# Transformer block, attention stage: the P·V matmuls are held back three steps behind the transposes instead of two

## The chip, the cores and the metric

The kernel runs on the 8 cores of one Trainium2 chip (trn2), every core with the same program and its own data. The time is the device time of the slowest core in microseconds (us), lower is better. Two cores share one batch element: each computes K and V for all 2048 positions of it, and the attention and feed-forward for its own 1024 rows (eight tiles of 128 rows).

## The reference, cut to what matters

```python
def reference(x, wq, wk, wv, wo, w_gate, w_up, w_down):   # x is [4, 2048, 2048]
    h = layernorm(x)
    q, k, v = (split_heads(h @ w.T) for w in (wq, wk, wv))  # 16 heads of 128
    scores = einsum('bhqd,bhkd->bhqk', q, k) / sqrt(128)
    scores = where(causal, scores, -inf)
    attn = softmax(scores)
    x = x + merge_heads(einsum('bhqk,bhkd->bhqd', attn, v)) @ wo.T
    h = layernorm(x)
    return x + (silu(h @ w_gate.T) * (h @ w_up.T)) @ w_down.T
```

## The kernel before, in words

The program is written as five lists of instructions, one for each engine, filled in the order in which the Python code runs. Each engine works its own list in order; an instruction that needs another engine's result is preceded by waits on a counter (`pe`, `dve`, `act`, and some for DMA). A wait for a value that the same engine has already waited for is left out (`Plan.wait`, L139 to L147).

The stages: layer norms, transposes and the Q projection up to about 353 us of the profile; attention from 353 to 1246 us; output projection and second layer norm to about 1370 us; gate and up projections to about 2240 us; down projection to the end.

The attention stage is a loop over 16 heads `h` (L567 to L586). Eight query tiles, called slots, form two groups. Group 0 (slots 0 to 3) sees up to 2048 keys, group 1 (slots 4 to 7) up to 1024. For a head the stage emits, in this order: scores and exponentials of the four slots of group 0; the K projection of the next head (64 matmuls); scores and exponentials of group 1; the V projection of the next head (64 matmuls) and its 16 transposes.

`emit_scores_softmax` (L430) does, for one slot, two or four score matmuls into PSUM banks A0, A1, B0, B1, adds masks by further matmuls (L449), and has ScalarE take the exponential of each pair of banks (L459, up to 1024 columns). A slot can write its scores only when the exponentials of the slot before have freed the banks.

What the change touches is `tpv_steps` (L496). It works on the exponentials of a group that was finished earlier. For each block `j` of 128 keys it makes a step:

- T(j): up to four matmuls of 128 columns (L513) that transpose and normalise the block for each slot, into PSUM bank C when j is even and D when j is odd. T(j) waits until that bank was emptied, that is for the eviction of step j-2 (`cd_free`).
- ev(j): one eviction of the bank into a buffer `pt`, by ScalarE when j is even (L522), by VectorE when j is odd (L526). There are four `pt` buffers, so ev(j) may start only when PV(j-4) has read the buffer (`pt_free`).
- PV(j): one matmul of up to 512 columns (L535), which adds the block's product with V into bank E (group 0) or F (group 1). PV(j) isn't emitted in its own step. It is put on the list `pend_pv`, and a later step emits it right behind its own transposes.

Group 0 has 16 steps (j from 0 to 15), group 1 has 8, and each ends with a `tail` that emits the PVs still held and one eviction of the result by VectorE (L547).

These steps are not run in one piece. They are drained between the scores of another group: of group 0's steps five behind each of slots 4 to 7 (L579), of group 1's steps three behind each of slots 0 to 3 of the next head (L570). So TensorE's order is scores of a slot, some steps, scores of the next slot, some steps. ScalarE's order has the exponentials of a slot ahead of the even evictions of the steps behind that slot. Only the last group 1 of the last head runs alone (L586).

There are 32 such groups: 16 group 0's, 15 group 1's between scores, and the last group 1.

Of the kernel before, what the change touches and what calls it, by code (L numbers as in the profile page):

```python
# [230 lines left out]
def emit_program(nc, P, sb, sbank, dr, phases=5):  # L231
# [3 lines left out]
    def bk(name, lo=0, hi=512):  # L235
        t, base = sbank[name]
        return t[:, base + lo: base + hi]
# [258 lines left out]
    def tpv_steps(h, g, slots):  # L496
        obank = "E" if g == 0 else "F"
        maxJ = JS[slots[0]]
        pend_pv = []
        steps = []  # L500

        def step_j(j):
            valid = [s for s in slots if JS[s] > j]
            nv = len(valid)
            jpar = j % 4
            bank = "C" if j % 2 == 0 else "D"

            t_pt = None
            for sl, s in enumerate(valid):
                w = [diag_tok[s], exp_tok[s]]  # L510
                if sl == 0:
                    w.append(cd_free[bank])
                t_pt = P.do("tensor", lambda e, s=s, j=j, sl=sl, bank=bank: e.matmul(  # L513
                    bk(bank, sl * 128, (sl + 1) * 128),
                    sb["p_sb"][:, P_OFF[s] + j * 128:P_OFF[s] + (j + 1) * 128],
                    sb["diag"][:, s, 0, :], start=True, stop=True), waits=w,
                    inc="pe" if sl == nv - 1 else None)
            for s in valid:
                p_region_free[s] = t_pt
                diag_free[s] = t_pt  # L520
            if j % 2 == 0:
                t_ev = P.do("scalar", lambda e, jpar=jpar, nv=nv, bank=bank: e.copy(  # L522
                    pt[jpar][:, 0:nv * 128], bk(bank, 0, nv * 128)),
                    waits=[t_pt, pt_free[jpar]], inc="act")
            else:
                t_ev = P.do("vector", lambda e, jpar=jpar, nv=nv, bank=bank: e.tensor_copy(  # L526
                    pt[jpar][:, 0:nv * 128], bk(bank, 0, nv * 128)),
                    waits=[t_pt, pt_free[jpar]], inc="dve")
            cd_free[bank] = t_ev
            w = [t_ev]  # L530
            if j == 0:
                w.append(ef_free[obank])

            def _pv(j=j, nv=nv, jpar=jpar, w=tuple(w)):
                t_pv = P.do("tensor", lambda e, h=h, j=j, nv=nv, jpar=jpar, obank=obank, maxJ=maxJ: e.matmul(  # L535
                    bk(obank, 0, nv * 128), vtm[h % 2][:, j, :],
                    pt[jpar][:, 0:nv * 128], start=(j == 0), stop=(j == maxJ - 1)),
                    waits=list(w), inc="pe")
                pt_free[jpar] = t_pv
            if len(pend_pv) >= 2:  # L540
                pend_pv.pop(0)()
            pend_pv.append(_pv)

        def tail():
            while pend_pv:
                pend_pv.pop(0)()
            t_oev = P.do("vector", lambda e, h=h, g=g, obank=obank: e.tensor_copy(  # L547
                sb["o_fm"][:, h, g * 512:(g + 1) * 512], bk(obank)),
                waits=[P.tok("pe")], inc="dve")
            ef_free[obank] = t_oev  # L550

        for j in range(maxJ):
            steps.append(lambda j=j: step_j(j))
        steps.append(tail)
        return steps
# [352 lines left out]
```

How the kernel before makes its waits and increments, by code:

```python
    def wait(self, eng, tok):  # L139
        sem, v = tok
        if v <= 0:
            return
        if self.waited[eng].get(sem, -1) >= v:
            return
        h = self.sems[sem]
        self.ops[eng].append(lambda e, h=h, v=v: e.wait_ge(h, v))
        self.waited[eng][sem] = v
# [1 line left out]
    def do(self, eng, build, waits=(), inc=None, k=1):  # L149
        for t in _flat(waits):
            self.wait(eng, t)
        if inc is not None:
            self.cnt[inc] += k
            h = self.sems[inc]
            self.ops[eng].append(lambda e, b=build, h=h, kk=k: b(e).then_inc(h, kk))
            return (inc, self.cnt[inc])
        self.ops[eng].append(lambda e, b=build: b(e))
        return None
```

## Time and profile before

| what | value |
|---|---|
| time before, median of 2 runs | 2916.1 us (2913.26 and 2918.93) |
| the profiled execution's own time | 2902.78 us |
| its span, slowest core (core 5) | 2900.5 us (the eight cores: 2890.1 to 2900.5) |
| TensorE matmul busy | 2450.0 us, 84% of the span |
| VectorE busy | 557.7 us, 19% |
| ScalarE busy | 551.8 us, 19% |
| PE's share of the chain that ended last | 79% |

The span runs from the first to the last instruction of one core. PE is TensorE's matmuls and PEld its weight loads, DVE is VectorE, ACT ScalarE, POOL GpSimd. A matmul's record covers its whole way through the array, so records of neighbouring matmuls overlap: two matmuls of 512 columns that follow each other start 0.22 us apart, though each record is 0.38 us long. A line such as "idle 0.17 <-ACT pt L522" says that the engine stood still for 0.17 us and that the ScalarE instruction of line 522 released it. The granted clock is TensorE's, as a share of 2.4 GHz.

### The profile page before, as it was taken

Reading aid. Unit: us, or ns where it says so; the run is one execution under the profiler, and the core shown is the slowest. Engines: PE = TensorE matmul, PEld = TensorE weight load, DVE = VectorE, ACT = ScalarE, POOL = GpSimd, SP = SyncE. Lnnn points to the kernel's source line nnn. Section 1 sums busy time; section 2 is a strip of 40 time slices with the busy share of each in tenths; the row PEclk is TensorE's granted clock in tenths of the full one; section 3 lists DMA queues with packets and bytes.
Section 4 is the critical chain, followed back from the end, with each engine's and each line's share of the span. In section 5 each row is a group of like instructions: output and inputs, shape, how many; then the busy total and the mean of one; then the engine's idle time right before and its main releaser. Section 6 shows DMA issues by size and latency. Waiting matters only on the chain.

```text
span 2900.5 us, 31994 instructions; the slowest of 8 cores (2890.1 to 2900.5 us)
## 1 busy us (share of the span) xinstructions
PE 2450.0 (84%) x12352; PEld 1143.0 (39%) x12352; DVE 557.7 (19%) x978; ACT 551.8 (19%) x1090; POOL 169.2 (6%) x324
## 2 busy tenths in 40 slices
PE   2676788878888888859779999999999999797796
PEld 1233344434444444414334444444444444343342
DVE  4322133333333333303300010001000100000000
ACT  4433223232333333302210000000000000000000
POOL 0000000000000000010000000000000011111110
PEclk9888999999999999958889999999999999898998
DMA  5333211111110101073244444444444445555554
GB/s 172 116 102 80 44 17 21 19 18 20 18 23 15 22 16 23 1 145 116 78 89 73 80 73 80 73 80 73 80 73 80 73 64 75 112 74 112 94 91 91
DMA packets 61491, 196.36 MB, mean 68 GB/s; under 512 B 6944, under 2 KB 6944, under 8 KB 56096
## 3 DMA queue, kind: packets, MB, share of 16 engines
q0 software_dynamic: 46080, 134.24, 28.5%
q1 hardware_dynamic: 15264, 60.07, 6.2%
q8 instruction: 103, 1.69, 0.2%
q14 instruction: 44, 0.36, 0.0%
HBM read 311.72 MB, written 16.78 MB: 113 GB/s over the span
## 4 chain that ended last, share of the span: by engine, by line
PE 79%; ACT 7%; DMA 5%; issue 4%; DVE 4%; SPq 0%; DVEq 0%; ACTq 0%; POOL 0%; POOLq 0%
PE psA L717 8%; PE psB L728 8%; PE psA L394 4%; PE psA L414 4%; PE psA L802 4%; PE psB L394 4%; PE psF L728 4%; PE psB L414 4%; PE psD L717 4%; PE psC L717 4%; PE psE L728 4%; PE psB L802 4%; PE psA L331 2%; DMA x2r<-x2s 2%; PE psB L331 2%
## 5 line engine op out<-in xcount | busy, mean ns | idle before, releaser
L459 ACT ACTIVATE p_sb<-psA,stats 128x1024 bf16<-128x1024 f32 (+3 forms) x128 | 132.4, 1034 | 559.2 <-PE psA L443 290.2
L717 PE MATMUL psA<-h_fm,wg 128*128 128x512 bf16 x1024 | 227.9, 381 | 8.9 <-issue 8.9
L728 PE MATMUL psB<-h_fm,wu 128*128 128x512 bf16 x1024 | 226.2, 379 | 0.0
L717 PE MATMUL psC<-h_fm,wg 128*128 128x512 bf16 x512 | 194.0, 379 | 0.0
L717 PE MATMUL psD<-h_fm,wg 128*128 128x512 bf16 x512 | 194.0, 379 | 0.0
L728 PE MATMUL psE<-h_fm,wu 128*128 128x512 bf16 x512 | 194.0, 379 | 0.0
L728 PE MATMUL psF<-h_fm,wu 128*128 128x512 bf16 x512 | 194.0, 379 | 0.0
L802 PE MATMUL psB<-wd,hidden 128*128 128x512 bf16 x512 | 155.4, 384 | 24.1 <-DVE osb L816 24.1
L802 PE MATMUL psA<-wd,hidden 128*128 128x512 bf16 x512 | 154.5, 383 | 5.6 <-DVE osb L816 3.8
L526 DVE CAST pt<-psD 128x512 bf16<-128x512 f32 x192 | 115.7, 602 | 210.2 <-PE psD L513 210.2
L717 PEld LDWEIGHTS psA<-h_fm,wg 128*128 128x128 bf16 x1024 | 100.7, 98 | 130.8 <-issue 11.3
L728 PEld LDWEIGHTS psB<-h_fm,wu 128*128 128x128 bf16 x1024 | 100.2, 98 | 120.8
L283 PE MATMUL psE<-eye,htm 128*128 128x128 bf16 x192 | 26.9, 290 | 138.1 <-DVE htm L266 131.2
L513 PE MATMUL psC<-diag,p_sb 128*128 128x128 bf16 x704 | 72.5, 221 | 74.8 <-ACT pt L522 72.5
L394 PE MATMUL psA<-h_fm,wkbuf 128*128 128x512 bf16 x512 | 122.1, 400 | 14.2 <-ACT p_sb L459 13.4
L746 DVE TENSOR_TENSOR hidden<-silu,psB 128x512 bf16<-128x512 bf16 x64 | 41.1, 683 | 422.6 <-PE psB L728 422.6
L414 PE MATMUL psA<-h_fm,wvbuf 128*128 128x512 bf16 x512 | 113.1, 379 | 6.3 <-ACT p_sb L459 6.3
L522 ACT CAST pt<-psC 128x512 bf16<-128x512 f32 x192 | 105.0, 547 | 63.4 <-PE psC L513 61.7
L394 PE MATMUL psB<-h_fm,wkbuf 128*128 128x512 bf16 x512 | 113.1, 379 | 0.0
L414 PE MATMUL psB<-h_fm,wvbuf 128*128 128x512 bf16 x512 | 113.1, 379 | 0.0
L739 ACT ACTIVATE silu<-psA 128x512 bf16<-128x512 f32 x64 | 34.7, 594 | 394.9 <-PE psA L717 394.9
L802 PE MATMUL psE<-wd,hidden 128*128 128x512 bf16 x256 | 98.2, 384 | 12.5 <-DVE osb L816 12.5
(124 smaller groups left out, 2985.4 us busy)
## 6 DMA issues: line engine op xcount, KB each, us to landing
wg<-wg_t POOLq DMA_DIRECT2D x64, 512.0 KB, 5.3
wu<-wu_t POOLq DMA_DIRECT2D x64, 512.0 KB, 5.4
wd<-wd_t POOLq DMA_DIRECT2D x128, 256.0 KB, 3.8
xt<-xkv SPq DMA_DIRECT2D x16, 1024.0 KB, 5.5
wqbuf<-wq_t POOLq DMA_DIRECT2D x16, 512.0 KB, 5.4
xt<-xq SPq DMA_DIRECT2D x8, 1024.0 KB, 10.1
wkbuf<-wk_t POOLq DMA_DIRECT2D x16, 512.0 KB, 5.1
wvbuf<-wv_t POOLq DMA_DIRECT2D x16, 512.0 KB, 5.0
```

What stands on the lines that cost most here:

```text
L331: t_mm = P.do("tensor", lambda e, h=h, sp=sp, c=c, bank=bank: e.matmul(bk(bank), sb["wqbuf"][:, c, :], sb["h1q"][:, c, sp * 512:(sp + 1) * ...
L394: t_mm = P.do("tensor", lambda e, h=h, sp=sp, c=c, bank=bank: e.matmul(bk(bank), sb["wkbuf"][:, c, :], sb["h1_fm"][:, c, sp * 512:(sp + 1) ...
L414: t_mm = P.do("tensor", lambda e, h=h, sp=sp, c=c, bank=bank: e.matmul(bk(bank), sb["wvbuf"][:, c, :], sb["h1_fm"][:, c, sp * 512:(sp + 1) ...
L459: t_exp = P.do("scalar", lambda e, s=s, slo=slo, shi=shi, sec=sec, sc_t=sc_t, sstat=sstat: e.activation(sb["p_sb"][:, P_OFF[s] + slo:P_OFF ...
L513: t_pt = P.do("tensor", lambda e, s=s, j=j, sl=sl, bank=bank: e.matmul(bk(bank, sl * 128, (sl + 1) * 128), sb["p_sb"][:, P_OFF[s] + j * 12 ...
L522: t_ev = P.do("scalar", lambda e, jpar=jpar, nv=nv, bank=bank: e.copy(pt[jpar][:, 0:nv * 128], bk(bank, 0, nv * 128)), waits=[t_pt, pt_fre ...
L526: t_ev = P.do("vector", lambda e, jpar=jpar, nv=nv, bank=bank: e.tensor_copy(pt[jpar][:, 0:nv * 128], bk(bank, 0, nv * 128)), waits=[t_pt, ...
L717: t_gmm = P.do("tensor", lambda e, hc=hc, c=c, half=half, par=par, gb=gb: e.matmul(bk(gb[half]), wg[par][:, c, :], sb["h2_fm"][:, c, half ...
L728: t_umm = P.do("tensor", lambda e, hc=hc, c=c, half=half, par=par, ub=ub: e.matmul(bk(ub[half]), wu[par][:, c, :], sb["h2_fm"][:, c, half ...
L739: t_silu[half] = P.do("scalar", lambda e, half=half, gb=gb: e.activation(sb["silu"][:, half * 512:(half + 1) * 512], bk(gb[half]), AF.Silu ...
L746: t_mul = P.do("vector", lambda e, hc=hc, half=half, ub=ub: e.tensor_tensor(sb["hidden"][:, hc, half * 512:(half + 1) * 512], sb["silu"][: ...
L802: t_mm = P.do("tensor", lambda e, qtr=qtr, hc=hc, tt=tt, par=par, bank=bank: e.matmul(bk(bank), sb["hidden"][:, hc, tt * 128:(tt + 1) * 12 ...
```

## The change

One constant of `tpv_steps`. A step that finds at least three held PVs (it was two) emits the oldest behind its own transposes.

```diff
--- before.py
+++ after.py
@@ -537,7 +537,7 @@
                     pt[jpar][:, 0:nv * 128], start=(j == 0), stop=(j == maxJ - 1)),
                     waits=list(w), inc="pe")
                 pt_free[jpar] = t_pv
-            if len(pend_pv) >= 2:
+            if len(pend_pv) >= 3:
                 pend_pv.pop(0)()
             pend_pv.append(_pv)
```

TensorE's list was T(0) T(1) T(2) PV(0) T(3) PV(1) ... and becomes T(0) T(1) T(2) T(3) PV(0) T(4) PV(1) ... The tail emitted two PVs and now emits three. No instruction is added or taken away on any engine, and no buffer.

## Rows read from the trace of the kernel before

**Rows 1.** Windows: the attention stage; busy us and count, then granted clock.

```profile
core 5: us, PE busy (x) PEld busy (x) DVE busy (x) ACT busy (x) POOL busy (x), PEclk, DMA share, GB/s
353.00:1246.00 893.00, 739.04 (x4532) 374.40 (x4532) 289.36 (x582) 299.19 (x576) 14.77 (x28) 0.98 0.10 18
```

**Rows 2.** Waits: who waited for whom, us in total, times, longest us.

```profile
ACT p_sb L459 <- PE psA L443: 290.2, 31, 31.0
PE psC L513 <- ACT pt L522: 72.5, 79, 2.0
PE psF L535 <- ACT pt L522: 21.7, 15, 1.4
PE psD L513 <- DVE pt L526: 8.7, 30, 0.3
```

**Rows 3.** Line 535 (all PVs): VectorE's share of what ended its idle time: us, times.

```profile
  DVE pt L526: 4.3, 16
```

**Rows 4.** Timeline of a group 1 between scores: start us, us long, engine, line.

```profile
809.14 0.39 PE L513 MATMUL psC<-diag,p_sb 128*128 128x128 bf16 x4
809.36 0.39 PE L513 MATMUL psD<-diag,p_sb 128*128 128x128 bf16 x4
...
811.67 0.38 PE L513 MATMUL psC<-diag,p_sb 128*128 128x128 bf16 x4 [1.92 <-ACT pt L522]
...
811.89 0.38 PE L535 MATMUL psF<-pt,vtm 128*128 128x512 bf16 x1
...
812.11 0.59 PE L443 MATMUL psA<-kfm,q_all 128*128 128x512 bf16 x2
812.15 0.59 ACT L522 CAST pt<-psC 128x512 bf16<-128x512 f32 x1 [0.62 <-PE psC L513]
...
812.80 1.11 ACT L459 ACTIVATE p_sb<-psA,stats 128x1024 bf16<-128x1024 f32 x1
...
813.19 0.39 PE L513 MATMUL psD<-diag,p_sb 128*128 128x128 bf16 x4
...
814.52 0.33 PE L513 MATMUL psD<-diag,p_sb 128*128 128x128 bf16 x3 [0.29 <-DVE pt L526]
...
814.89 0.58 ACT L522 CAST pt<-psC 128x512 bf16<-128x512 f32 x1
814.90 0.59 PE L443 MATMUL psA<-kfm,q_all 128*128 128x512 bf16 x2
...
815.59 1.11 ACT L459 ACTIVATE p_sb<-psA,stats 128x1024 bf16<-128x1024 f32 x1
...
818.08 0.34 PE L535 MATMUL psF<-pt,vtm 128*128 128x256 bf16 x2 [1.45 <-ACT pt L522]
```

**Rows 5.** Timeline of a group 0 between scores, TensorE alone.

```profile
836.96 0.38 PE L513 MATMUL psC<-diag,p_sb 128*128 128x128 bf16 x4 [1.53 <-ACT pt L522]
...
837.39 0.39 PE L513 MATMUL psD<-diag,p_sb 128*128 128x128 bf16 x4
...
838.16 0.38 PE L513 MATMUL psC<-diag,p_sb 128*128 128x128 bf16 x4 [0.17 <-ACT pt L522]
...
847.65 0.22 PE L535 MATMUL psE<-pt,vtm 128*128 128x128 bf16 x1 [0.20 <-DVE pt L526]
848.28 4.04 PE L414 MATMUL psA<-h_fm,wvbuf 128*128 128x512 bf16 x18 [0.42 <-ACT p_sb L459]
```

**Rows 6.** Timeline of the last group 1, which runs alone, TensorE.

```profile
1240.59 0.58 PE L513 MATMUL psC<-diag,p_sb 128*128 128x128 bf16 x4 [0.40 <-ACT pt L522]
...
1241.39 0.63 PE L513 MATMUL psD<-diag,p_sb 128*128 128x128 bf16 x4
```

**Rows 7.** Timeline of ScalarE in another head: slot 2's first exponential.

```profile
471.46 1.11 ACT L459 ACTIVATE p_sb<-psA,stats 128x1024 bf16<-128x1024 f32 x1 [1.06 <-PE psA L443]
```

**Rows 8.** Windows behind a group 1, columns as in rows 1.

```profile
527.00:532.80 5.80, 3.45 (x24) 1.87 (x25) 1.54 (x3) 4.66 (x11) 0.00 (x0) 0.95 0.00 0
532.80:538.60 5.80, 5.80 (x21) 2.33 (x22) 1.76 (x7) 0.62 (x2) 0.00 (x0) 0.75 0.01 3
```

## The prediction, made before the changed kernel was run

> **What bounds the kernel now.** I read the page first: TensorE is busy for 84% of the span and makes up 79% of the chain that ended last, so what counts is TensorE's idle time and what stands in front of it. The windows by stage come second. The change lies in the attention stage alone, 893 us long, in which TensorE is busy for 739 us at a granted clock of 0.98 [rows 1]. About 154 us of it are TensorE standing still. The other stages run the same instructions as before.
>
> The view of waits comes third and says where it stands still [rows 2, 3]. The transposes T(j) wait for ScalarE's evictions 79 times, 72.5 us, and for VectorE's 30 times, 8.7 us: 81.2 us. The PV matmuls wait 15 times for ScalarE, 21.7 us, and 16 times for VectorE, 4.3 us: 26.0 us. So a PV waits in 31 places, about once in each of the 32 groups, though there are 384 PVs. Since each group has one wait, it must be the tail, and the timeline shows it: PV(6) of a group 1 after 1.45 us of standing still, PV(15) of a group 0 after 0.20 us [rows 4, 5].
>
> That is the first thing to see. In the middle of a group a PV never waits for its eviction. T(j) needs PSUM bank C or D, and has therefore already waited for ev(j-2). PV(j-2), which follows it, finds its input ready. TensorE works its list in order, so while T(j) stands still nothing behind it can go. The lists before and after differ in which PV follows a transpose, not in what a transpose waits for.
>
> Here a rule of the Trainium skill speaks against the change. "Perfetto Trace Analysis", section "Optimization Strategy", says that a bubble that comes back again and again can mean too little SBUF or PSUM for the next tile. The trace agrees: 81.2 us of such bubbles stand in front of T and are released by the evictions that empty banks C and D. By that rule a longer list of held PVs gives nothing, and a third bank would be needed.
>
> **The change part by part.** It adds and removes nothing. Each group has one PV fewer early (between T(2) and T(3)) and one more late (in the tail). Between them all PVs come one step later. I price one PV of 512 columns at 0.22 us, the distance from its start to that of the next instruction (811.89 to 812.11), and one T of four matmuls at the same 0.22 us (809.14 to 809.36, two T in a row with nothing between them, which is what T(2) T(3) becomes) [rows 4].
>
> *Group 0, 16 times.* Before: T(2) at 836.96, PV(0), T(3) at 837.39, PV(1), T(4) at 838.16 after 0.17 us of idle [rows 5]. After: T(2) at 836.96, T(3) at 837.18 (its bank's eviction began behind T(1) and is over), PV(0), and then T(4), which waits for ev(2). ev(2) hangs on T(2) alone, which hasn't moved, so T(4) stays at 838.16 and the idle before it grows from 0.17 to 0.39 us. Behind T(4) one PV follows as before, so the scores of slot 5 and all else come when they did. In the tail there is one more PV of 512 columns in front of PV(15). PV(15) waits 0.20 us for ev(15), and the V projection that follows waits 0.42 us more for slot 7's exponential (848.28) [rows 5]. The 0.22 us fall into these. Sum: 0.
>
> *Group 1 between scores, 15 times.* T(0) T(1) T(2) are drained behind slot 0, and PV(0) leaves this place, so the scores of slot 1 start at 811.89 and not 812.11. Their exponential gains nothing: it starts at 812.80 because ev(2), ahead of it on ScalarE, ends at 812.74 (812.15 + 0.59) [rows 4]. But TensorE now runs 0.22 us early. T(3) goes from 813.19 to 812.97, ev(3) with it, T(5), which waits for ev(3), from 814.52 to 814.30, and the scores of slot 2 from 814.90 to 814.68. The exponential of slot 2 starts at 815.59. Its scores end at 814.90 + 0.59 = 815.49, and ev(4) ahead of it on ScalarE ends at 814.89 + 0.58 = 815.47. ScalarE went on 0.06 us behind ev(2), so by ScalarE alone it could start at 815.53. The gain is capped at 0.06 us. From there ScalarE is in charge (two exponentials, ev(6)), and PV(6) waits for ev(6) as before (818.08). The additional PV of the tail lies inside the 1.45 us of idle, which the early lead of 0.22 us would have lengthened. Then scores of slot 3, their exponential and the K projection, all 0.06 us earlier. Sum: 15 x 0.06 = 0.9 us gained.
>
> In one head slot 2's exponential was truly late: ScalarE stood idle for 1.06 us before it [rows 7]. There the 0.22 us come through in full, 0.2 us more. Of the 31 times that L459 waited for L443 [rows 2] this is the only one at slot 2; the others are a head's first exponential and slot 3's.
>
> *The last group 1.* It runs alone and at half clock (T and PV 0.43 us). T(3) moves up from 1241.39 to about 1241.0, T(4) then stands about 0.2 us for ev(2), and the tail, which had no idle, can't give it back [rows 6]. Sum: 0.2 us lost.
>
> *Waits and queues.* No wait is added. ev(j) waits for PV(j-4), to have its `pt` buffer free. Before, PV(j-4) stood behind T(j-2); now it stands behind T(j-1), that is directly in front of T(j), for which ev(j) waits anyway. The four buffers are just enough. DMA issues wait for projections, which move by 0.06 us.
>
> The sum is -0.9 - 0.2 + 0.2 = -0.9 us. The profiled execution took 2902.78 us, so it would be 2901.9. It lies 13 us under the median of the runs shown, 2916.1, and against that the sum gives **2915 us**.
>
> Bounds of the unknown parts. If PV(0)'s place were on the path in full in all 31 groups between scores: -31 x 0.22 = -6.8 us. If the tail's additional PV were never covered: +6.8 us. A PV leaves one place and enters another in every group, so I take the value near zero that the rows give.
>
> The clock is the larger unknown. In the stage it is 0.98, so 2% of 893 us or 18 us are lost to stretches at the lower level. Cut into windows of 5.8 us, 16 of 154 show less than 1.00, in eight places. One of these, behind a group 1, shows 0.95 and then 0.75 [rows 8]. Such a fall costs (0.05 + 0.25) x 5.8 = 1.7 us. They come behind groups 1, where TensorE is busy for 3.45 of 5.8 us, but not in every head. The change moves idle time by 0.22 us within a group, without adding to it. I take no change and keep -18 us (no fall left) and +18 us (twice as many) as its bounds.
>
> **The rivals.**
>
> *The held PVs fill the waits, as a longer lookahead is meant to.* If all PV waits went, 26 us: 2890 us. If those of T went too, 107 us: 2809 us, 3.7% faster. For it: the tail's waits are real, and one more ready PV now stands in front of them. Against it: what that PV covers at the end it leaves open at T(3) or T(4), and T waits for a bank. Chance 3% for the first, 1% for the second.
>
> *The clock falls more often.* The idle before T(4) grows from 0.17 to 0.39 us in every group 0. With 18 us more: 2933 us. With a fall of 1.7 us in each of the 31 groups: 2968 us. Over 2%, 58 us, it takes 34 falls, more than there are groups. Against it: behind a longer stop of 1.53 us group 0's matmuls ran on at full pace (T(2) and PV(0) in 0.43 us) [rows 5]. Chance 6%, and 5% for the other sign, down to 2897 us.
>
> On this the Trainium skill, page "TensorE: Matmul & The Clock Gate", section "A second HAM failure mode: psum-queue depth-cycling", says that short stops between groups of matmuls can make the clock swing between its levels. The trace has both, and the change shifts such stops without lengthening their sum.
>
> *The ring of four buffers is too short (the slower side).* If ev(j) came to wait for a PV emitted behind T(j), each of the 256 evictions from j = 4 on would start one PV later: 256 x 0.22 = 56 us, 2972 us, 1.9% slower. It decides from a distance of four steps on. With three, PV(j-4) still stands in front of T(j). Chance 2%.
>
> **How the numbers follow.** The forecast, no change that can be told, has 80%; the rivals 4, 6, 5 and 2%; 3% stay for what I don't see. A measurement of this kernel can tell about 2%, 58 us, from no change. Only the second half of the first rival lies beyond it on the fast side; on the slow side only worse forms of the ring or the clock: faster 1%, within 2% 97%, slower 2%. The range is 2915 us and 13 us to both sides, the distance between the profiled execution and the median, which also takes in the 6.8 us and most of the clock's 18: 2901 to 2929.
>
> **What would show it.** In the profile of the changed kernel T(3) starts 0.22 us behind T(2) in every group. The idle of T for evictions rises from 81 to about 85 us (16 x 0.22 more in front of T(4)), that of PVs for VectorE falls to about 1 us, and that of PVs for ScalarE stays near 22 us. The attention stage stays 893 us long within 2 us. I am wrong if the waits of T fall by tens of us, if evictions are released by L535, or if the stage's clock leaves 0.97 to 0.99.

## The result and the profile after

The change made the kernel slower by a quarter of a per cent: median 2923.3 us against 2914.2 us, ratio 1.0024 with a 95% interval of 1.0012 to 1.0036. (The chip sometimes lowers the clock of a whole die; such executions are in these two medians and left out of every ratio and mean here.) The profiled execution took 2909.99 us, its span is 2907.6 us on core 0, and the eight cores' spans lie between 2895.2 and 2907.6 us, where before they lay between 2890.1 and 2900.5.

The forecast was 2915 us, no change that can be told and a shade faster. The time, 2923.3 us, lies in its range, but the change is clear of noise and goes the other way.

The stage first. Windows of the changed kernel, core 0 (busy us and count by engine, granted clock, DMA share, GB/s):

```profile
core 0: us, PE busy (x) PEld busy (x) DVE busy (x) ACT busy (x) POOL busy (x), PEclk, DMA share, GB/s
353.00:1246.00 893.00, 735.14 (x4416) 373.46 (x4503) 286.50 (x576) 295.91 (x573) 14.77 (x28) 0.97 0.10 18
```

The clock is 0.97 where it was 0.98 [rows 1]. (Both programs have the same matmuls; the counts, 4416 and 4532, differ because records are missing from the trace, so the busy times aren't compared.) The waits of the same core (waiting instruction, releaser, us in total, times, longest):

```profile
ACT p_sb L459 <- DVE kfm L399: 214.8, 14, 15.9
...
PE psC L513 <- ACT pt L522: 77.6, 81, 2.0
...
PE psF L535 <- ACT pt L522: 18.5, 15, 1.2
```

T waits 5 us more for ScalarE and PV 3 us less [rows 2], and in the records of line 535 VectorE's 4.3 us [rows 3] are gone. That is what a matmul moved from the front of a group to its tail does. The first line is new to the story: ScalarE's wait for the K projection, 7.0 us more than before (core 5):

```profile
ACT p_sb L459 <- DVE kfm L399: 207.8, 14, 15.9
```

Its rows one by one, before (core 5) and after (core 0), in ScalarE's timeline. Each row is the first exponential of four slots; "17.33 <-PE" is the first of group 0, behind the V projection, "<-DVE kfm" the first of group 1, behind the K projection:

```profile
808.75 1.11 ACT L459 ACTIVATE p_sb<-psA,stats 128x1024 bf16<-128x1024 f32 x1 [17.33 <-PE psA L443]
835.13 1.11 ACT L459 ACTIVATE p_sb<-psA,stats 128x1024 bf16<-128x1024 f32 x1 [14.20 <-DVE kfm L399]
865.36 1.11 ACT L459 ACTIVATE p_sb<-psA,stats 128x1024 bf16<-128x1024 f32 x1 [17.33 <-PE psA L443]
893.52 1.11 ACT L459 ACTIVATE p_sb<-psA,stats 128x1024 bf16<-128x1024 f32 x1 [15.87 <-DVE kfm L399]
```

```profile
809.68 1.11 ACT L459 ACTIVATE p_sb<-psA,stats 128x1024 bf16<-128x1024 f32 x1 [17.33 <-PE psA L443]
837.41 1.11 ACT L459 ACTIVATE p_sb<-psA,stats 128x1024 bf16<-128x1024 f32 x1 [15.76 <-DVE kfm L399]
867.64 1.11 ACT L459 ACTIVATE p_sb<-psA,stats 128x1024 bf16<-128x1024 f32 x1 [17.33 <-PE psA L443]
895.40 1.11 ACT L459 ACTIVATE p_sb<-psA,stats 128x1024 bf16<-128x1024 f32 x1 [15.80 <-DVE kfm L399]
```

A head has two sides. The K side runs from the first kind of row to the second, the V side from the second to the next first. The K side before takes 835.13 - 808.75 = 26.4 us with a wait of 14.20, and 893.52 - 865.36 = 28.2 us with a wait of 15.87. The second is a head in which TensorE's clock fell to half behind a group 1, so that the projection, which starts here at about 877 us, ran slowly for a while (before, core 5; the window of 2 us ahead of these shows 1.00):

```profile
877.00:879.00 2.00, 1.99 (x5) 0.70 (x6) 1.04 (x6) 0.65 (x2) 0.00 (x0) 0.51 0.00 0
879.00:881.00 2.00, 2.00 (x7) 0.77 (x6) 0.04 (x1) 0.00 (x0) 0.00 (x0) 0.64 0.00 0
```

I measured all sides of all eight cores in this way, 14 K sides and 15 V sides a core:

| kernel | K sides with a fall | K side, full clock / with a fall | V sides with a fall | V side, full clock / with a fall | all 30 sides, mean of 8 cores |
|---|---|---|---|---|---|
| before | 54 of 112 | 26.39 / 27.95 us | 2 of 120 | 30.23 / 31.73 us | 857.3 us |
| after | 79 of 112 | 26.17 / 27.81 us | 21 of 120 | 30.23 / 31.45 us | 862.0 us |

(The table's durations are medians. The 30 sides are these 29 and the first K side, which has no group 1.) So a head at full clock became 0.22 us shorter, 14 x 0.22 = 3.1 us a core, and the clock fell more often. The falls cost (54 x 1.56 + 2 x 1.50) / 8 = 10.9 us a core before and (79 x 1.64 + 21 x 1.22) / 8 = 19.4 us after. 8.5 us lost less 3.1 us gained is 5.4 us; the sides differ by 4.7 us. Of the 8.5 us, 5.7 are K sides and 2.8 are V sides.

These counts are from one execution of each kernel, and its cores aren't independent: in before, five of the eight show a fall in the very same heads. What bears them out over many executions is the granted clock of the whole program, below.

The V side's falls are nearly new: 21 where there were 2. One in the changed kernel, core 0, TensorE's timeline from T(2) of a group 0 on, and the windows over it:

```profile
433.30 0.38 PE L513 MATMUL psC<-diag,p_sb 128*128 128x128 bf16 x4 [1.53 <-ACT pt L522]
433.52 0.39 PE L513 MATMUL psD<-diag,p_sb 128*128 128x128 bf16 x4
433.74 0.38 PE L535 MATMUL psE<-pt,vtm 128*128 128x512 bf16 x1
...
434.50 0.38 PE L513 MATMUL psC<-diag,p_sb 128*128 128x128 bf16 x4 [0.38 <-ACT pt L522]
```

```profile
431.00:434.90 3.90, 1.99 (x24) 1.34 (x23) 1.80 (x3) 2.26 (x4) 0.53 (x1) 1.00 0.62 98
434.90:438.60 3.70, 3.48 (x20) 2.31 (x20) 0.79 (x2) 2.27 (x4) 0.00 (x0) 0.54 0.20 39
```

T(3) follows T(2) by 0.22 us, and the pause ahead of T(4) is 0.38 us where it was 0.17 [rows 5], just as the working had it. Right behind it the granted clock is 0.54, TensorE's lower level of 1.2 GHz for nearly the whole window.

### The profile page after: what moved, and what is told of

It reads as the page before. It is cut to its first block, busy times and chain, and to the rows that moved or that the text cites. A ratio compares the mean times of both kernels' runs of the same rounds, so it can differ in the third digit from the quotient of the medians.

```text
span 2907.6 us, 31738 instructions; the slowest of 8 cores (2895.2 to 2907.6 us)
## 1 busy us (share of the span) xinstructions
PE 2437.7 (84%) x12111; PEld 1143.3 (39%) x12352; DVE 558.0 (19%) x978; ACT 549.9 (19%) x1090; POOL 169.2 (6%) x324
## 4 chain that ended last, share of the span: by engine, by line
PE 78%; ACT 7%; DMA 5%; issue 4%; DVE 4%; SPq 0%; DVEq 0%; ACTq 0%; POOL 0%; POOLq 0%
PE psA L717 8%; PE psB L728 8%; PE psA L394 4%; PE psF L728 4%; PE psD L717 4%; PE psA L414 4%; PE psA L802 4%; PE psB L802 4%; PE psB L394 4%; PE psB L414 4%; PE psC L717 4%; PE psE L728 4%; DMA x2r<-x2s 2%; ACT p_sb L459 2%; PE psA L331 2%
## 5 line engine op out<-in xcount | busy, mean ns | idle before, releaser
L717 PE MATMUL psA<-h_fm,wg 128*128 128x512 bf16 x1004 | 227.8, 382 | 10.8 <-DMA wg<-wg_t 9.6
L717 PE MATMUL psC<-h_fm,wg 128*128 128x512 bf16 x491 | 186.1, 379 | 0.0
L728 PE MATMUL psE<-h_fm,wu 128*128 128x512 bf16 x491 | 186.1, 379 | 0.0
L394 PE MATMUL psA<-h_fm,wkbuf 128*128 128x512 bf16 x502 | 128.5, 417 | 14.7 <-ACT p_sb L459 13.4
L513 PE MATMUL psC<-diag,p_sb 128*128 128x128 bf16 x704 | 72.3, 221 | 80.5 <-ACT pt L522 77.6
L522 ACT CAST pt<-psC 128x512 bf16<-128x512 f32 x192 | 105.0, 547 | 63.0 <-PE psC L513 61.3
L802 PE MATMUL psC<-wd,hidden 128*128 128x512 bf16 x246 | 94.6, 385 | 12.9 <-DVE osb L816 12.9
```

What stands on the lines that cost most here:

```text
L394: t_mm = P.do("tensor", lambda e, h=h, sp=sp, c=c, bank=bank: e.matmul(bk(bank), sb["wkbuf"][:, c, :], sb["h1_fm"][:, c, sp * 512:(sp + 1) ...
L717: t_gmm = P.do("tensor", lambda e, hc=hc, c=c, half=half, par=par, gb=gb: e.matmul(bk(gb[half]), wg[par][:, c, :], sb["h2_fm"][:, c, half ...
L728: t_umm = P.do("tensor", lambda e, hc=hc, c=c, half=half, par=par, ub=ub: e.matmul(bk(ub[half]), wu[par][:, c, :], sb["h2_fm"][:, c, half ...
L802: t_mm = P.do("tensor", lambda e, qtr=qtr, hc=hc, tt=tt, par=par, bank=bank: e.matmul(bk(bank), sb["hidden"][:, hc, tt * 128:(tt + 1) * 12 ...
```

## The experiments

Two theories. *Clock*: the new order itself gains 0.22 us a head; the loss comes from more falls of TensorE's clock. *Path*: the order costs time by itself, and the falls are incidental. If it is the clock, it is still open what calls for it: the 0.2 us more of pause ahead of T(4), the tail, or where a head lies in time. "Mean core span" is the mean over the eight cores of all executions that enter the ratio, with its standard error; it is less noisy than the slowest core's time, by which the ratios go. The changed kernel's is 2903.0 +-0.6 us; before's was 2894.2, 2893.2 and 2895.9 us (all +-0.6 or less) in the three sets of runs, each on another chip. Falls are again counted in one execution of each kernel. The granted clock of the whole program, a mean over the same executions as the spans (errors of 0.0007 or less; the kernels are those of the sections below), tells the same story:

| kernel | granted clock, whole program |
|---|---|
| before, three sets | 0.9465, 0.9462, 0.9458 |
| the changed kernel | 0.9414 |
| two held, filled (two sets) | 0.9509, 0.9507 |
| three held, filled (two sets) | 0.9506, 0.9511 |
| group 0 alone | 0.9426 |
| group 1 alone | 0.9459 |
| whole change, T(4) filled | 0.9469 |
| held to T(4) only | 0.9425 |
| three held late | 0.9430 |
| a head 0.22 us longer | 0.9486 |
| faster than both | 0.9509 |

### Taking the falls away

Idle matmuls in TensorE's pauses, into the PSUM bank (E or F) that the stretch doesn't use. Nothing reads them.

```diff
+    def fill(bank, n, cols=512):
+        for _ in range(n):
+            P.do("tensor", lambda e, bank=bank, cols=cols: e.matmul(
+                bk(bank, 0, cols), eye[:, :], sb["h1_fm"][:, 0, 0:cols],
+                start=True, stop=True), waits=[ef_free[bank]])
...
             pend_pv.append(_pv)
+            if j == 1 and not solo:
+                fill(fbank, 6 if g == 0 else 7)
...
             while pend_pv:
+                if len(pend_pv) == 2 and g == 1 and not solo:
+                    fill(fbank, 5)
                 pend_pv.pop(0)()
...
         emit_combine(h, 0)
         if h + 1 < NH:
+            fill("E", 3)
```

(`fbank` is F in group 0 and E in group 1, `solo` the last group 1. In kernels with these lines L513 becomes L521, L522 L530 and L535 L543; L498 is the idle matmul.) With two PVs held:

> Two PVs held as before the change, and idle matmuls (128x512, into the PSUM bank that the stretch does not use) in TensorE's pauses: 7 behind T(1) of a group 1, 5 ahead of PV(6), 3 ahead of each K projection, 6 behind T(1) of a group 0. Clock theory (the change is slower because the clock falls in more heads, 11 of 14 K sides in its trace against 7 before, 1.6 us each): no K side is longer than 27 us here, the stage's clock is 1.00, and the time is about 10 us below before (7 falls x 1.6), 2904. Path theory (the new order itself costs time; the clock is incidental): the fillers change nothing, 2914, or cost a few us where they are in the way.

With three:

> Three PVs held, and the same idle matmuls. Clock theory: all falls are gone, and what is left of the change is its gain in heads at full clock, 26.2 against 26.4 us on the K side: 15 x 0.2 = 3 us less than d2_warm, about 2901. Path theory: 7 to 9 us more than d2_warm.

Both were run again in another set:

> The kernel with two PVs held and idle matmuls in the pauses, a second time, as the partner of the next two. No falls in the attention stage; mean core span about 9 us below before.

> Three PVs held and idle matmuls in the pauses, a second time. Order alone, with no falls: K sides of 26.17 us against 26.39, so the attention stage is 3 us shorter than with two held, and the mean core span too (within its noise of about 1 us).

| kernel | ratio to before, 95% interval | mean core span | K falls | V falls | K side | all sides |
|---|---|---|---|---|---|---|
| two held, filled | 0.9955 (0.9938 to 0.9973) | 2884.9 +-0.8 us | 0 | 0 | 26.39 us | 846.3 us |
| three held, filled | 0.9974 (0.9951 to 0.9996) | 2882.9 +-1.2 us | 0 | 0 | 26.17 us | 843.3 us |
| two held, again | 0.9953 (0.9923 to 0.9982) | 2885.7 +-1.0 us | 0 | 0 | 26.39 us | 846.3 us |
| three held, again | none (only two executions count) | 2881.6 +-1.1 us | 0 | 0 | 26.17 us | 843.4 us |

No side falls in any core. The pauses filled are seen in TensorE's timeline of three held, filled, core 3. T(2) stood for 1.92 us before; now seven idle matmuls run and 0.41 us are left:

```profile
408.57 1.67 PE L498 MATMUL psE<-h_fm,eye 128*128 128x512 bf16 x7
410.66 0.38 PE L521 MATMUL psC<-diag,p_sb 128*128 128x128 bf16 x4 [0.41 <-ACT pt L530]
```

And the order alone, with no fall in either, is 3 us shorter with three held (846.3 to 843.3 us, and 846.3 to 843.4 in the second set). The path theory, which wanted 7 to 9 us more, is out. The sums close as well: the falls cost 857.3 - 846.3 = 11.0 us before and 862.0 - 843.3 = 18.7 us after the change, 7.7 us more, and 7.7 less the 3.0 of order is the 4.7 us by which the sides differ. By the slowest core's time this 3 us doesn't show: the two kernels' intervals overlap, with three held even on the higher side in the first set. Its profiled execution took 2921.35 us, and its slowest core had a granted clock of 0.78 ahead of the attention stage (up to 353 us) and of 1.00 within it, so that time wasn't lost in the attention stage. The mean core spans lean the way of the 3 us (2.0 and 4.1 us, each with an error of about 1.5, the second with only two executions of three held).

### Which group

```diff
-            if len(pend_pv) >= 2:
+            if len(pend_pv) >= (3 if g == 0 else 2):
```

> Three PVs held in group 0 only, two in group 1. If the longer pause ahead of T(4) of group 0 (0.17 to 0.39 us) is what lowers the clock: slower than before by 6 to 9 us, with heads at full clock 26.4 + 30.2 us. If it is group 1: as before, 2914.

The other kernel has `(3 if g == 1 else 2)`.

> Three PVs held in group 1 only, two in group 0. If group 1 (26.2 us on the K side at full clock, and longer rows of heads with a fall) is the cause: slower than before by 6 to 9 us. If it is group 0: 2 to 3 us faster than before, by 0.2 us a head.

| kernel | ratio, 95% interval | mean core span | K falls | V falls | all sides |
|---|---|---|---|---|---|
| group 0 alone | 1.0020 (1.0005 to 1.0035) | 2902.3 +-0.5 us | 48 of 112 | 53 of 120 | 863.7 us |
| group 1 alone | 1.0015 (0.9996 to 1.0034) | 2894.7 +-1.5 us | 59 of 112 | 1 of 120 | 855.1 us |

Group 0 brings the V sides' falls and 8.1 us of mean core span (2902.3 against 2894.2), group 1 the 0.22 us (K side 26.17 us) and no loss of span (+0.5 +-1.5). I had expected either the full loss or 2 to 3 us of gain from group 1. In the profiled execution its sides are 2.2 us shorter (855.1 against 857.3), with 59 K falls against 54; over all executions no gain shows, and where it went isn't shown.

### The pause ahead of T(4)

The whole change, plus one idle matmul of 0.22 us in that pause:

```diff
-            if len(pend_pv) >= 2:
+            if len(pend_pv) >= 3:
...
+            if g == 0 and j == 4:
+                fill("F", 1)
             t_pt = None
             for sl, s in enumerate(valid):
```

> Three PVs held in both groups, and one idle matmul of 512 columns (0.22 us) in the pause ahead of T(4) of every group 0, which brings TensorE's idle time there back from 0.39 to 0.17 us. Pause theory (the 0.22 us more of idle there is what lowers the clock in group 0's stretch): V sides with a fall go from 21 of 120 in the changed kernel, and 53 in the one with group 0 alone, back to about 2, and the mean span of the cores goes from 2903 to about 2894. Order theory (the falls come from the shifted order or from the head's length, not from this pause): the falls stay, the time stays near the changed kernel's, 1.002 of before.

Measured: V falls 0 of 120, K falls 60 of 112, all sides 855.0 us, mean core span 2890.0 +-0.8 us against 2893.2 +-0.6 of before in the same set, ratio 0.9993 (0.9978 to 1.0009). TensorE's timeline of core 5:

```profile
430.36 0.38 PE L521 MATMUL psC<-diag,p_sb 128*128 128x128 bf16 x4 [1.53 <-ACT pt L530]
430.58 0.39 PE L521 MATMUL psD<-diag,p_sb 128*128 128x128 bf16 x4
430.80 0.38 PE L543 MATMUL psE<-pt,vtm 128*128 128x512 bf16 x1
431.02 0.38 PE L498 MATMUL psF<-h_fm,eye 128*128 128x512 bf16 x1
431.56 0.38 PE L521 MATMUL psC<-diag,p_sb 128*128 128x128 bf16 x4 [0.17 <-ACT pt L530]
```

and the window over this and the following:

```profile
428.00:435.60 7.60, 5.49 (x54) 3.35 (x53) 3.25 (x5) 4.92 (x9) 0.53 (x1) 1.00 0.42 69
```

T(4) starts 1.20 us behind T(2), as in the changed kernel (434.50 - 433.30). Nothing on the path moved; only 0.22 us of idle time became busy, once in each of 16 heads. That took all of the V side's falls away, and the loss with them. The K falls too are 60 here, as good as the 59 of group 1 alone, where the changed kernel had 79. The K sides' part of the cost was 5.7 of 8.5 us, so much of what the pause cost seems to come out on K sides; how a pause on a V side brings a fall behind the next group 1 these runs don't show. The changed kernel itself wasn't run again in this set; each is compared with its own before, 1.0024 and 0.9993, and the two intervals don't overlap.

The same from the other side: three held from T(3) to T(4) only, and two again from T(5) on, so that the tail is as before.

```diff
-            if len(pend_pv) >= 2:
+            if len(pend_pv) >= (2 if g == 1 or j > 4 else 3):
                 pend_pv.pop(0)()
+            if g == 0 and j == 5:
+                pend_pv.pop(0)()
```

> Group 1 as before. Group 0 holds three PVs only from T(3) to T(4) and emits two behind T(5), so that all from there on, the tail too, is as before. Pause theory: the pause ahead of T(4) is 0.39 us, so V sides fall as in the kernel with group 0 alone (53 of 120) and the mean core span is about 8 us above before. Tail theory (what counts is the longer tail or the shift of all PVs): as before.

Measured: V falls 71 of 120, K falls 28 of 112, mean core span 2903.5 +-0.5 us (+10.3), ratio 1.0041 (1.0027 to 1.0056). Core 1, TensorE, and the two windows of 3.7 us from the first exponential of the side on:

```profile
493.26 0.38 PE L513 MATMUL psC<-diag,p_sb 128*128 128x128 bf16 x4 [0.38 <-ACT pt L522]
```

```profile
490.20:493.90 3.70, 1.79 (x21) 1.11 (x19) 1.38 (x2) 2.42 (x5) 0.31 (x1) 0.96 0.71 118
493.90:497.60 3.70, 3.70 (x21) 2.07 (x19) 0.69 (x1) 2.03 (x4) 0.00 (x0) 0.58 0.14 28
```

With the pause there and the tail as before, the falls stay. The tail theory is out for the V sides.

### Where a head lies in time

Three held late in group 0, from T(9) on, with the early part as before:

```diff
-            if len(pend_pv) >= 2:
+            if len(pend_pv) >= (3 if g == 0 and j >= 9 else 2):
```

> Group 1 as before. Group 0 holds two PVs up to T(8) and three from T(9) on, the tail included. Pause theory: V sides fall in 2 to 5 of 120, as before; the held PV(7) moves behind the scores of slot 6, whose exponential found ScalarE idle for 0.9 us, so a V side at full clock gets shorter by up to 0.2 us, 3 us in all. Tail theory: V sides fall in some 50 of 120 and the mean core span is 8 us above before.

And before itself, with a head made 0.22 us longer by one matmul more on TensorE's path:

```diff
+                if c == 0 and sp == 0 and h > 0:
+                    for _ in range(1):
+                        P.do("tensor", lambda e, bank=bank: e.matmul(
+                            bk(bank, 0, 512), sb["wkbuf"][:, 0, :],
+                            sb["h1_fm"][:, 0, 0:512],
+                            start=True, stop=True), waits=w)
+                    w = []
```

> Two PVs held as before; each K projection (from the second head on) starts with one more matmul of 512 columns, on TensorE's path, so that a head is 0.22 us longer and all pauses are the same. If the falls depend only on the pauses: K sides fall in 54 of 112 as before, V sides in 2 of 120, and the kernel is 15 x 0.22 = 3.3 us slower. If they depend also on how long a head is (where it lies in time against the chip's own rhythm): the number of falls changes by more than 15, either way, and the time by more than 5 us from that.

| kernel | ratio, 95% interval | mean core span | K falls | V falls | K / V side, full clock | a head with a K fall |
|---|---|---|---|---|---|---|
| three held late | 1.0039 (1.0022 to 1.0056) | 2900.7 +-0.9 us | 98 of 112 | 0 of 120 | 26.39 / 30.01 us | 57.99 us |
| a head 0.22 us longer | 1.0000 (0.9980 to 1.0021) | 2893.3 +-0.6 us | 26 of 112 | 1 of 120 | 26.60 / 30.23 us | 58.39 us |

"Three held late" is a miss of both theories. The V side has no fall and is 0.22 us shorter, as the pause theory said, but the kernel is 7.5 us slower, because nearly every K side falls, though group 1 wasn't touched. Core 5, ScalarE:

```profile
574.77 1.11 ACT L459 ACTIVATE p_sb<-psA,stats 128x1024 bf16<-128x1024 f32 x1 [17.33 <-PE psA L443]
602.79 1.11 ACT L459 ACTIVATE p_sb<-psA,stats 128x1024 bf16<-128x1024 f32 x1 [15.84 <-DVE kfm L399]
632.79 1.11 ACT L459 ACTIVATE p_sb<-psA,stats 128x1024 bf16<-128x1024 f32 x1 [17.33 <-PE psA L443]
660.96 1.11 ACT L459 ACTIVATE p_sb<-psA,stats 128x1024 bf16<-128x1024 f32 x1 [15.70 <-DVE kfm L399]
```

Head after head 58.0 us apart (632.79 - 574.77), each with a slow K projection. The kernel with a longer head does 3.3 us more work on the path, leaves every pause as it was, and has half as many falls as before (26 against 54), so that the time is the same. Of the two marks set, the falls passed theirs (more than 15), and the time, 3.3 us under the forecast, not its own (more than 5 us). Falls come in rows of heads that follow each other, and the rows are the longer the nearer a head with a fall is to 58.0 us. All kernels that have falls, K sides and V sides apart:

| kernel, side that falls | head with such a fall (both sides) | falls | longest row of heads |
|---|---|---|---|
| a head 0.22 us longer, K | 58.39 us | 26 of 112 | 2 |
| before, K | 58.18 us | 54 of 112 | 5 |
| held to T(4) only, K | 58.18 us | 28 of 112 | 4 |
| group 0 alone, K | 58.15 us | 48 of 112 | 4 |
| group 1 alone, K | 58.04 us | 59 of 112 | 10 |
| the changed kernel, K | 58.04 us | 79 of 112 | 7 |
| whole change, T(4) filled, K | 58.01 us | 60 of 112 | 10 |
| three held late, K | 57.99 us | 98 of 112 | 14 |
| held to T(4) only, V | 58.05 us | 71 of 120 | 10 |
| group 0 alone, V | 57.82 us | 53 of 120 | 7 |
| the changed kernel, V | 57.62 us | 21 of 120 | 2 |

The three rows of V sides have the same pause ahead of T(4) and differ in the length of a head, which may be why they have 21, 53 and 71 falls. So the longer pause brings falls on V sides, and how often they come depends also on how long a head is, within tenths of a microsecond. Why 58.0 us is a bad length isn't shown by these runs. The table is one profile of each kernel, and it has equal or nearly equal lengths with 54 and 28, 59 and 79, 60 and 98 falls, so the length isn't all of it.

### A version faster than both

The pauses filled as above, three held in group 1, and three held from T(9) on in group 0:

```diff
-            if len(pend_pv) >= 2:
+            if len(pend_pv) >= (3 if g == 1 or j >= 9 else 2):
```

> Idle matmuls in the pauses; three PVs held in group 1, and in group 0 from T(9) on. If the gains at full clock add (0.22 us on the K side from group 1, 0.22 us on the V side from the PV that moves behind slot 6's scores): K sides 26.17, V sides 30.01, no falls, attention stage 840 us against 843.3 with three held everywhere and 846.3 with two, and about 0.994 to 0.995 of before. If the falls come back in spite of the idle matmuls: above 846.

Measured: 0.9940 of before (0.9921 to 0.9960), mean core span 2879.3 +-0.5 us against 2895.9. No falls, K side 26.17, V side 30.01, all sides 840.1 us. The gains of both groups add once the clock stays up. Its idle matmuls cost no one a wait. The profile of line 498, core 0 (counts, durations, and then two lists of who waited, both empty):

```profile
L498 PE MATMUL psE<-h_fm,eye x225: 379/379/379, 355.3 to 1196.8; 128*128 128x512 bf16 x113
...
L498 PE MATMUL psF<-h_fm,eye x96: 379/379/379, 370.9 to 1203.2; 128*128 128x512 bf16 x96
its engine sat idle before it (us, times) until:
who waited for it (us, times):
```

## Why the prediction was wrong, step by step

*What T and PV wait for: right in kind.* T was forecast to wait 85 us in all, and waited 88.4 (77.6 for ScalarE, 10.8 for VectorE). PV's wait for VectorE is gone (about 1 us was forecast). Its wait for ScalarE was to stay near 22 us and came out as 18.5: in the groups shown, PV(6)'s idle of 1.45 us [rows 4] became 1.23 (core 0, 414.43), since the tail's third PV fills 0.22 us of it. The forecast of the longer lookahead filling the waits, 26 or 107 us of gain, didn't come. The bubbles ahead of T are still there, released by the evictions of banks C and D.

*Group 0 at full clock, sum 0: right.* V sides take 30.23 us before and after. T(3) 0.22 us behind T(2), T(4) in place with 0.38 us of idle ahead of it.

*Group 1, 0.06 us a head: right mechanism, wrong size.* It is 0.22 us, the whole PV. What failed here is the cap: I took it that slot 1's exponential gains nothing, because the eviction ahead of it ends 0.06 us before it, and that slot 2's can start no nearer than 0.06 us behind the end of the eviction ahead. The changed kernel shows otherwise (core 0, TensorE and ScalarE, from slot 0's exponential to slot 2's):

```profile
405.31 1.11 ACT L459 ACTIVATE p_sb<-psA,stats 128x1024 bf16<-128x1024 f32 x1 [17.33 <-PE psA L443]
...
408.44 0.59 PE L443 MATMUL psA<-kfm,q_all 128*128 128x512 bf16 x2
408.70 0.58 ACT L522 CAST pt<-psC 128x512 bf16<-128x512 f32 x1 [0.62 <-PE psC L513]
...
409.18 1.12 ACT L459 ACTIVATE p_sb<-psA,stats 128x1024 bf16<-128x1024 f32 x1
...
411.24 0.59 PE L443 MATMUL psA<-kfm,q_all 128*128 128x512 bf16 x2
...
411.93 1.11 ACT L459 ACTIVATE p_sb<-psA,stats 128x1024 bf16<-128x1024 f32 x1
```

The eviction's record ends at 408.70 + 0.58 = 409.28, and the exponential's begins at 409.18, 0.10 us earlier. ScalarE's records overlap. Counted from slot 0's exponential (808.75 before, 405.31 here), slot 1's starts 3.87 us later instead of 4.05, and slot 2's 6.62 instead of 6.84: they gain 0.18 and 0.22 us. The rows of before held the hint [rows 4]: both exponentials start 0.69 us behind the start of their scores (812.11 to 812.80, 814.90 to 815.59). What held them was their scores, and the 0.06 us behind the eviction was chance. 14 x 0.22 = 3.1 us of gain instead of 0.9.

*The clock: this is the step that failed.* The prediction said: "The change moves idle time by 0.22 us within a group, without adding to it. I take no change". The runs show +7.7 us of falls in place of that nothing (18.7 against 11.0), 8.5 by the counts. The sum of idle time is not what decides. Its place does: the 0.22 us were added to the pause of 0.17 us ahead of T(4), which follows closely on that of 1.53 us ahead of T(2); TensorE had been busy for 1.99 of 3.90 us when its clock fell. One idle matmul there is the difference between 21 of 120 V sides with a fall, and none. The evidence that I gave against it, a T(2) and a PV at full pace right behind a stop of 1.53 us, shows only that this one stop is survived. The bounds of 18 us were too wide as well: all falls of before cost 11.0 us. Of the 18.7 us that the prediction's 16 windows add up to, 6.8 lie from 1217 us on, in the last head.

The rival that named it had the mechanism and the place right, "the idle before T(4) grows from 0.17 to 0.39 us in every group 0", and a price too far off (18 us where the falls cost 8.5 us more) and a chance of 6%. It would have deserved the likeliest place beside no change, since the trace of before already showed falls in half the K sides. Of the 25 more K falls (79 against 54) 19 go when the pause ahead of T(4) is filled. That the head's length has a part in their number, as the section on it suggests, the prediction had no notion of.

The Trainium skill, page "TensorE: Matmul & The Clock Gate", section "A second HAM failure mode: psum-queue depth-cycling", says that short stops between groups of matmuls can make the clock go up and down. The runs agree, and say how little it takes here: 0.22 us in a head of 56.4 us.

*The ring of four buffers and the last group: nothing in the runs speaks of a cost there.* No eviction of the changed kernel waits longer than before for a PV (0.8 us in one case, 1.7 us in two before). The last group's 0.2 us was too small to test. The 56 us set against a distance of four were never run, and they misread the code: `pt_free` is looked up when ev(j) is emitted. With four held, PV(j-4) is emitted only behind that, so ev(j) would wait for PV(j-8) and could overwrite a buffer that PV(j-4) has yet to read. That is a wrong result, not a wait.

*The total.* -0.9 us was forecast in place of -3.0 us of order and +7.7 us of falls, +4.7 us in the attention stage of the profiled executions. That the time still lies in the range is owed to its width, 13 us to each side, and not to the mechanism.

## What to carry to other kernels

Where the profile shows TensorE's granted clock falling at some repetitions of a loop and not at others, price an edit there by what it does to the pauses, place by place, before pricing it by its order. Count the falls of all cores, repetition by repetition; a mean clock of 0.98 hides them. Idle matmuls in pauses that were there anyway delayed nothing here and took such falls away: they were worth 0.45% with the old order, and 0.6% together with an order that is shorter at full clock. Differences of 0.2 to 0.4% between two orders can be falls alone; idle matmuls in both kernels show what the order itself is worth.

## What the runs showed of the hardware that was not expected

- 0.22 us of idle matmul a head, in a pause of 0.38 us that stayed the same length on the path, took the V sides' falls from 21 of 120 to none and the K sides' from 79 of 112 to 60, and the mean core span from 2903.0 to 2890.0 us (measured on two chips; the ratios to before are 1.0024 and 0.9993).
- A kernel with 3.3 us more work on TensorE's path took the same time as before (ratio 1.0000), with half as many K falls in its profile (26 against 54); one with 0.22 us less a head, three held late, took 0.4% longer, with 98.
- ScalarE's next record begins 0.10 us before the one ahead of it ends (409.18 against 409.28), so the ends in a timeline are no lower bound for the next start.
